# Low parts of a split matmul on another engine, one load moved ahead, the last column sums by TensorE, and one small load behind the last stores

## The reference

```
aggr  = segment_sum(x[src], dst) / max(count, 1)
h     = aggr @ W_l.T + b_l + x @ W_r.T
mu    = mean(h, axis=0); var = mean((h - mu)**2, axis=0)      # over all 50000 rows
h2    = relu((h - mu) * rsqrt(var + 1e-5) * gamma + beta)
out   = layernorm(x + h2, axis=-1)
```

## Time and profile before

| | |
|---|---|
| time of the runs shown | 2512.76 us median of 3 (2511.4 to 2515.43) |
| time of the profiled execution | 2514.4 us |
| its span | 2512.7 us, mean granted TensorE clock 0.85 |
| busy: PE, DVE, ACT, POOL | 1728.9, 1949.2, 1471.4, 1434.9 us |
| DMA | 752.91 MB, mean 300 GB/s |

### The profile page before, as it was taken

The page is one execution under the profiler, slowest core; times in us unless marked ns, Lnnn a source line. Parts: engine busy times, 40 slices in busy tenths (PEclk is TensorE's granted clock), DMA queues, the critical chain, the costliest instruction groups (busy, mean ns, idle before and its releaser), DMA issues.

```text
span 2512.7 us, 29785 instructions
## 1 busy us (share of the span) xinstructions
PE 1728.9 (69%) x9404; PEld 1406.2 (56%) x9404; DVE 1949.2 (78%) x3455; ACT 1471.4 (59%) x2847; POOL 1434.9 (57%) x696
## 2 busy tenths in 40 slices
PE   7999999999999999999999999998100000000000
PEld 6778888888888888888888888886000000000000
DVE  7736888888888788888888888887587777766666
ACT  4333554555455544555455545553389998878787
POOL 5255555555656555665555565556296556556554
PEclk9999999999999999999999999999555555555555
DMA  5467888888888888888888888887999999999998
GB/s 190 145 208 216 265 269 266 261 252 276 264 274 243 273 275 246 271 267 269 256 263 256 270 273 268 254 265 192 412 394 425 426 426 426 426 426 422 413 419 343
DMA packets 125535, 752.91 MB, mean 300 GB/s; under 512 B 20809, under 2 KB 20809, under 8 KB 65726
## 3 DMA queue, kind: packets, MB, share of 16 engines
q1 hardware_dynamic: 71710, 618.44, 65.3%
q0 software_dynamic: 53664, 132.51, 20.9%
HBM read 515.32 MB, written 246.22 MB: 303 GB/s over the span
## 4 chain that ended last, share of the span: by engine, by line
PE 54%; DMA 22%; ACT 10%; DVE 7%; POOL 3%; issue 3%; SPq 0%; DVEq 0%; ACTq 0%; POOLq 0%
PE pd L568 11%; PE pd L570 11%; PE pd L569 11%; DMA out<-hx 9%; DMA hx<-h_scratch 5%; ACT hx L925 5%; ACT hx L915 4%; DMA raw<-xT_whole 3%; DMA h_scratch<-zz,si 3%; POOL hx L1443 2%; PE px L673 2%; PE pz L673 2%; PE pz L674 2%; PE pz L675 2%; PE px L674 2%
## 5 line engine op out<-in xcount | busy, mean ns | idle before, releaser
L568 PE MATMUL pd<-wc_hi,x_hi 128*128 128x512 f32 x1564 | 626.6, 401 | 23.0 <-DVE wc_lo L961 15.3
L781 ACT ACTIVATE h_out<-pd 128x512 f32<-128x512 f32 x391 | 233.7, 598 | 663.9 <-PE pd L570 641.6
L570 PE MATMUL pd<-wc_hi,x_lo 128*128 128x512 f32 x1564 | 613.4, 392 | 0.0
L569 PE MATMUL pd<-wc_lo,x_hi 128*128 128x512 f32 x1564 | 611.1, 391 | 0.0
L1443 POOL TENSOR_TENSOR hx<-hx,scale_b 128x2560 f32<-128x2560 f32 (+2 forms) x91 | 439.9, 4844 | 289.3 <-DMA hx<-h_scratch 242.6
L1421 POOL DMA_INDIRECT h_scratch<-zz,si x156 | 321.5, 2061 | 418.7 <-DVE xe_lo L1119 189.8
L568 PEld LDWEIGHTS pd<-wc_hi,x_hi 128*128 128x128 f32 x1564 | 294.6, 188 | 81.9 <-issue 16.3
L925 ACT ACTIVATE hx<-hx,nr,rs 128x512 f32<-128x512 f32 x385 | 279.9, 802 | 87.2 <-DVE nr L1294 87.2
L570 PEld LDWEIGHTS pd<-wc_hi,x_lo 128*128 128x128 f32 x1564 | 294.1, 188 | 64.4
L569 PEld LDWEIGHTS pd<-wc_lo,x_hi 128*128 128x128 f32 x1564 | 295.1, 189 | 57.9
L1371 POOL DMA_INDIRECT xn<-x,gi x156 | 294.5, 1888 | 47.7 <-issue 44.0
(11 more groups left out here) (231 smaller groups left out, 3256.9 us busy)
## 6 DMA issues: line engine op xcount, KB each, us to landing
raw<-xT_whole SPq DMA_DIRECT2D x78, 1280.0 KB
h_scratch<-h_out SPq DMA_DIRECT2D x78, 1280.0 KB
hx<-x SPq DMA_DIRECT2D x78, 1280.0 KB, 20.6
hx<-h_scratch SPq DMA_DIRECT2D x77, 1280.0 KB, 15.4
out<-hx SPq DMA_DIRECT2D x77, 1280.0 KB, 18.1
hs<-h_scratch SPq DMA_DIRECT2D x76, 1280.0 KB
h_out<-h_scratch SPq DMA_DIRECT2D x2, 1280.0 KB, 10.2
xn<-x,gi POOLq DMA_INDIRECT x156
```

The costliest lines, as they stand in the source:

```text
L568: pe.matmul(pd[i][0:n, :], hi, wc["hi"][:, kc, :], start=kc == 0, stop=False)
L569: pe.matmul(pd[i][0:n, :], hi, wc["lo"][:, kc, :], start=False, stop=False)
L570: last = pe.matmul(pd[i][0:n, :], lo, wc["hi"][:, kc, :], start=False, stop=kc == KC - 1)
L781: act.activation(h_out[0:n, b, t, :], pd[(b + t) % 2][0:n, :], ACT.Copy).then_inc(s_ev, 1)
```

## The change

Five edits, all in the order of work; no tile or matmul of the main loops changes its form.

1. The low parts of groups 5 to 8 go from POOL to DVE (group 4 was there already): groups 5, 6 and 7 at three places in DVE's front chain, group 8 (FRONT) in turn -2, behind the one-hot tables of turn 0.
2. `load2(0, 1)`, h and x of group 0 of stage two, is issued in turn 75, before the read-back of group 73, instead of turn 77; group 1's stays in turn 77.
3. The squares of groups 76, 77 and 78 are no longer added to `acc2` by DVE. PE sums their rows directly with the ones matrix into the same bank, after the five tiles of `acc2` and before the five of `acc1`. In turn 79 DVE takes the squares of group 75 ahead of the sums of group 76. `s_done` waits for PE's sums (`s_sqs`).
4. The load of h of group 78 goes from behind the store of group 70 to behind the store of group 73.
5. POOL works groups 75 and 76 of stage two tile by tile as well.

```diff
@@ lo_by_dve / lo_by_pool, product()
-            return KC * g - KC * FRONT + KC + 1
-        def lo_by_pool(g):
-            return KC * g + KC - KC * (g > MIDDLE)
+            return KC * g - KC * MIDDLE + KC + 1
-                    if isinstance(g, int) and g == MIDDLE:
-                        pe.wait_ge(s_xld, KC + 1)
-                    elif isinstance(g, int) and g <= FRONT:
-                        pe.wait_ge(s_xlp, lo_by_pool(g) if g > 0 else 1)
+                    if isinstance(g, int) and g < MIDDLE:
+                        pe.wait_ge(s_xlp, KC * g + KC if g > 0 else 1)
                     else:
-                        pe.wait_ge(s_xlp, lo_by_pool(FRONT))
                         pe.wait_ge(s_xld, lo_by_dve(g))
@@ scales(k)
-            return [(t, t + 1) for t in range(tiles_in(k))] if k < 2 or fine(k) else [(0, tiles_in(k))]
+            return [(t, t + 1) for t in range(tiles_in(k))] if k < 2 or k >= G - 3 else [(0, tiles_in(k))]
@@ SP, turns
+                    if u == U - REACH:
+                        sp.wait_ge(s_dm, TG * G + 1)
+                        load2(0, 1)
                     if sums_at(u + 1) is not None:
                         load_sums(sums_at(u + 1))
...
-                        sp.wait_ge(s_dm, TG * G + 1)
-                        load2(0, EARLY2)
+                        load2(1, EARLY2)
@@ SP, stage two
-                if k >= 1 and k - 1 + NB2 <= G:
+                if k >= 1 and k - 1 + NB2 < G:
                     load2_h(k - 1 + NB2)
+                if k == G - NB2 + 4:
+                    load2_h(G)
@@ PE, between the stages
+                pe.wait_ge(s_a2, G - 2)
+                for t in range(TG):
+                    pe.matmul(pd[1][:], ones_ff[:], acc2[:, t, :], start=t == 0, stop=False)
+                for g in range(G - 2, G + 1):
+                    n = rows_in(g)
+                    for t in range(tiles_in(g)):
+                        pe.wait_ge(s_sq, TG * g + t + 1)
+                        last = pe.matmul(pd[1][:], ones_ff[0:n, :], sums_of(g)[0:n, t, :], start=False, stop=g == G)
+                last.then_inc(s_sqs, 1)
                 pe.wait_ge(s_a1, G)
                 sum_columns(0, acc1, range(1, TG))
-                pe.wait_ge(s_a2, G)
-                sum_columns(1, acc2, range(1, TG))
                 pe.wait_ge(s_a1, G + 1)
-                sum_columns(0, acc1, (0,))
-                pe.wait_ge(s_a2, G + 1)
-                sum_columns(1, acc2, (0,)).then_inc(s_bs, 1)
+                sum_columns(0, acc1, (0,)).then_inc(s_bs, 1)
@@ DVE, front and turns
+            def x_lows_of(g):
+                for kc in range(KC):
+                    x_low(g, g % 2, kc)
...
             dve.tensor_scalar(rel[a, :, HW[0]:HOTS]..., srel[:, H1:WIN], float(P), None, ALU.subtract)
+            x_lows_of(MIDDLE + 1)
...
             dve.tensor_reduce(cov[a, 0:1], seen[a], AX.XY, ALU.add)
+            x_lows_of(MIDDLE + 2)
             dve.wait_ge(s_xrank, 1)
...
             dve.memset(psl[:], 0.0).then_inc(s_ct, 1)
+            x_lows_of(MIDDLE + 3)
...
+                    if u == -EARLY:
+                        x_lows_of(FRONT)
...
+                    if u == U + 1:
+                        take_squares(sums_at(u - 1))
                     if sums_at(u) is not None:
                         take_sums(sums_at(u))
-                    if u >= U:
+                    if u == U:
                         take_squares(sums_at(u - 1))
...
-                take_squares(G)
                 dve.wait_ge(s_a1, G + 1)
-                dve.wait_ge(s_a2, G + 1)
+                dve.wait_ge(s_a2, G - 2)
+                dve.wait_ge(s_sqs, 1)
@@ POOL, front
-            for g in range(2, FRONT + 1):
-                for kc in range(KC if g != MIDDLE else 0):
+            for g in range(2, MIDDLE):
+                for kc in range(KC):
                     x_low(g, g % 2, kc)
```

More of the change, by code:

```diff
@@ L62, in bass_sage_batchnorm_residual_layernorm_kernel @@
     assert D == KC * P and KC * P == 512 and 0 < LAST <= P and N + 2 * P < EMPTY and HALF <= 512
-    assert G % 2 == 0 and (G - FRONT) % 2 == 0 and WIN * EB >= PW and G > FRONT + 8 and NB2 < G - 2
+    assert G % 2 == 0 and (G - FRONT) % 2 == 0 and WIN * EB >= PW and G > FRONT + 8 and FRONT == MIDDLE + 4 and NB2 < G - 2
     CW = D + 8
@@ L284, in bass_sage_batchnorm_residual_layernorm_kernel @@
                                              "stored", "squared", "taken")]
+        s_sqs = sem("last_squares_summed")
         s_done, s_bs, s_b1, s_b2, s_bnr = (sem(n) for n in (
@@ L1038, in _ @@
                 dve.scalar_tensor_tensor(vals[a, :, :, k], v, 256.0, vd, ALU.subtract, ALU.mult)
-            for kc in range(KC):
-                x_low(MIDDLE, MIDDLE % 2, kc)
+            x_lows_of(MIDDLE)
             for k, v in enumerate((dlo, slo)):
```

## The result

The changed kernel took 2502.6 us (median of 8, 2496.8 to 2507.31) against 2512.77 (median of 8, 2510.07 to 2515.43): ratio 0.9955, 95% interval 0.9947 to 0.9964, 11.3 us by the ratio, where 15.0 were forecast. It is spread wider than the kernel before, and the profiled execution (2496.8 us, span 2495.1) is the fastest of the eight. So its 17.6 us are not what the change is worth; a second profile of the same kernel (span 2496.9) and those of the variants are read beside it.

A forecast was written before the change was run, and what follows sets the result against it. The prediction took PE to bound stage one and DMA stage two. Front 7.5, between the stages 3.5 and end 4.0 summed to 15.0 us saved, giving a median of 2497.8 us, range 2491.5 to 2505.0.

The forecast's parts named there:

- the front: Stage one's first groups: DVE's low parts shorten PE's waits ahead of groups 5 and 7, saving 7.5 us (5.5 to 8.3).
- the middle: Between the stages: moved early load 2.2 us plus DVE's and PE's sums 1.3, together 3.5 us (-3 to 8.8).
- the end: Last groups of stage two: tile by tile scaling lets ACT normalise group 75 sooner, saving 4.0 us (2 to 4.5).
- case (a): Whole kernel: all terms as forecast, 2494 to 2501 us, chance 0.61.
- rival (b): Between the stages: early load delays the chain its full 6.2 us, PE's sums gain nothing; 2501 to 2504.5 us, chance 0.17.
- I take it as full: Front: PE's clock stays full behind the shortened wait ahead of group 5, saving 1.65 us.
- The loss taken for the chain ahead, 4.0 us: Between the stages: the early load's new place delays scatters and loads due meanwhile by 0 to 6.2 us, 4.0 taken.
- PE's part: Between the stages: PE's added squares nearly eat what DVE gives, leaving 0 to 2.6 us gained, 1.3 taken.
- the row: Between the stages: last scatter, issued at 1761.31, landed at 1771.65 behind 5.24 MB, suggesting delay by nearly the whole load.
- In time that is nothing by itself: End: stores of 71 to 73 leave 10.1 us sooner, gaining no time since the engines' chain bounds it.
- lands near 2492: End: group 78's h, behind three stores (9.3 us) from about 2482, lands before DVE needs it near 2495 or 2496.
- Rival (d): End: held by group 78's load or the last stores, gaining 2.0 us instead of 4.0; 2499.8 us, chance 0.06.

The follow-up runs named there:

- second series: The changed kernel run again with no edit, against the kernel before: 2500.13 us, ratio 0.995.
- One store less: Changed kernel with h of group 78 loaded behind the store of 71, and group 74's store left out: 2498.8 us, ratio 0.9934 to the kernel before.
- behind store 70 again: Changed kernel with h of group 78 loaded behind the store of group 70, as in the kernel before: 2501.6 us, ratio 0.9952.
- behind store 71: Changed kernel with h of group 78 loaded behind the store of group 71 instead of 73: 2500.23 us, ratio 0.9951 to the kernel before.

## Why the prediction was right, and which step was wrong

The forecast of a faster kernel held and the time lay in the range. Of the terms of the sum the front is right within its bounds, the middle was taken too low and the end failed; the middle's surplus of some 2.5 us made up for a part of the end's missing 4.0, which is luck. 2502.6 us lie outside the 2494 to 2501 of case (a) and inside those of rival (b), but what (b) says did not happen: the middle gave most of its gain. The second series, 2500.13, lies in (a)'s.

**Front, 7.5 us (5.5 to 8.3).** Alone 7.3 by the ratio (4.3 to 10.3); by load 9 4.1 to 7.1 against the one profile before, and 6.5 by the means. The wait ahead of group 7 went whole, as worked out, and the one ahead of group 5 shrank. Two sizes were off. DVE came at 98.62 as the bound said, not sooner, and its four took 3.23 us, so PE waited 2.7 us and not 1.8 to 2.4. And "I take it as full" for the clock was true in three of seven: 2.7 us of idle time lie where the clock sometimes falls, though in the kernel before 3.18 us left it alone. That is a step where both outcomes happen in the same program, and the term should have been their mean.

**Between the stages, 3.5 us (-3 to 8.8).** The two profiles of the changed kernel show 7.3 and 5.2 us, the eight with both edits 6.0 on average, the early load alone 5.5 by its ratio (3.3 to 7.8). The loss taken for the chain ahead, 4.0 us, was the mis-sized term: it measured some 1.5. The full 6.2 us came out behind it (scatter and read-back together 19.3 without the early load, 12.8 with it). PE's part, "0 to 2.6 us", measured 2.4 and 0.7 in the changed kernel, and -0.6 to 2.4 over the eight.

The Trainium skill ("DMA: Bandwidth & Descriptors", Queues, rings and completion order) has a DMA engine take in turn the queues that have work. The estimate worked out from it, a delay of 2 to 3 us, was nearer to the measured 1.5 than the 4.0 that I took from the row. The runs show only the size, not the mechanism.

**End, 4.0 us (2 to 4.5).** Failed; it measured 0. The step was "In time that is nothing by itself, since the chain is the engines'; it keeps DMA from becoming the bound". The engines' part was right (4 us sooner, where nothing else stood in the way), but DMA's 25 us of work behind the landing of group 76 and the wait for the last landing are a limit of the same length: relieving one of the two leaves the other. One store less shows it. I had the bytes in the same windows and did not add them up against the engines' time.

**Group 78's load, "lands near 2492" (10 us behind its issue).** It took 17.1 us, from 2464.74 to 2481.83, and held ACT for 5.2 us and the last DVE instruction for 4.0 (29.2 against 25.2). The step counted only the three stores. The load took 7.4 us with none of them ahead of it in the kernel before, 8.4 behind store 70 again and 11.2 behind store 71; in the changed kernel the second piece of h of group 77 landed only at 2469.3, and the store of 70 was ahead too. 7.4 and the forecast's own 9.3 make 16.7. Rival (d), held end, is what happened, with a chance of 0.06; it took off all 4.0 us of the end and not 2.0.

**Turns.** Taken as passing the front's gain on. They did not lose it, and the profiles show more, which stays open. From load 9 to the last whole load it takes 1526.0 us on average in the five profiles with the old front (1524.8 to 1527.5) and 1523.8 in the nine with edit 1 (1522.0 to 1526.4). So the 4.1 us of the profiled execution are mostly scatter, but that some 2 us belong to edit 1 is not excluded.

**Sum.** By the profiles' means: front 6.5, middle 6.0, stage two 0.3, end 0, and 2.2 in the turns. By the medians the kernel gained 11.3 us (9 to 13.3) and 12.6 in the second series. The five edits alone add up to some 15 us by their ratios; their intervals are 2 to 3 us wide to either side, so no interaction can be read from that.

## What to carry to other kernels

At an end where stores drain, add up the DMA time of all that is still to pass and set it beside the engines' chain; if they are within a few us, an edit on one of them gives nothing. For a small load behind stores, count everything that is still ahead of it, and start from what it takes today (7.4 us here with no held store ahead). When PE idles 2.4 to 3.2 us ahead of a group, count the clock's loss as a coin toss (it fell in six of the twelve such waits here), and rather remove the wait: moving four instructions two steps sooner in DVE's list did it here. A bulk load is best put where the DMA share is low and the bytes are not yet wanted: 2.62 MB out of a saturated stretch gave over 6 us there and took some 1.5 where it went.

## What was not expected of the hardware

- The same idle time of PE (2.67 and 2.68 us, and 3.58 and 3.62 ahead of the column sums) was followed by a granted clock of 0.50 in one execution and by full clock in another of the same program.
- In some executions PE idles 2.1 us in group 8, 1.4 us of it at an instruction that waits for nothing that the profile shows. The cause is open.
- In the ten us ahead of the landing of group 76 DMA is busy at a share of 0.85 to 1.01 but moves only 301 to 347 GB/s in the profiles read for it, against 422; loading group 77 in one piece did not change it.
